# ScalarE makes the D skip of a Mamba-2 mixer in slot 6 of its own chunk instead of slot 3 of the next

## What is computed

```python
zxbcdt = xn @ in_proj_w
z, xBC, dt = split(zxbcdt)                 # 512, 512 + 2*128, 32
dt = softplus(dt + dt_bias)
xBC = silu(causal_conv1d(xBC, conv_w, conv_b))
x_ssm, Bm, Cm = split(xBC)                 # 32 heads of 16
y = ssd_scan(xh, dt, Bm, Cm, A)            # h = h*exp(dt*A) + dt*x*B;  y = h @ C
y = y + D_skip[None, None, :, None] * xh   # the D skip
y = y * silu(z)
y = y * rsqrt(mean(y*y) + 1e-5) * rms_w
return y @ out_proj_w
```

## Time and profile before

| | us |
|---|---|
| median of 3 runs | 3185.61 (3182.48 to 3186.94) |
| the profiled execution, time | 3180.88 |
| the profiled execution, span | 3179.2 |
| PE busy | 2799.2 (88%) |
| DVE busy | 1839.9 (58%) |
| ACT busy | 1384.6 (44%) |
| POOL busy | 678.1 (21%) |
| mean granted clock of PE | 0.943 |

### The profile page before, as it was taken

One profiled execution on the slowest core, in us unless ns is written; L12 is line 12 of the kernel. 1 busy time (PEld: TensorE's weight loads), 2 busy tenths in 40 slices (PEclk: granted clock), 3 DMA queues, 4 the chain that ended last, 5 costly groups with the idle time before them and its releaser, 6 DMA issues. The chain is left out here.

```text
span 3179.2 us, 46142 instructions
## 1 busy us (share of the span) xinstructions
PE 2799.2 (88%) x16998; PEld 2086.3 (66%) x16998; DVE 1839.9 (58%) x3504; ACT 1384.6 (44%) x2394; POOL 678.1 (21%) x716
## 2 busy tenths in 40 slices
PE   0488888888888888869999799999999999999999
PEld 0354555455555555458888687887878787878787
DVE  4688888888888888746767433333333333333332
ACT  0566666666666666536555322222222222222221
POOL 5022222222222222210000122222222222222221
PEclk6799989998999899879999899999999999999999
DMA  3010101010101010035211100000000000000000
GB/s 125 29 35 20 35 20 35 20 35 20 35 21 35 21 35 11 28 104 208 70 62 64 48 13 7 11 14 16 14 16 14 16 14 16 14 16 14 16 14 8
DMA packets 104858, 107.06 MB, mean 34 GB/s; under 512 B 35897, under 2 KB 98617, under 8 KB 102977
## 3 DMA queue, kind: packets, MB, share of 16 engines
q1 hardware_dynamic: 99520, 103.81, 10.1%
q10 hardware_dynamic: 5120, 0.19, 0.1%
HBM read 71.41 MB, written 40.94 MB: 35 GB/s over the span
## 5 line engine op out<-in xcount | busy, mean ns | idle before, releaser
L1597 PE MATMUL fbank<-hid,fw 128*128 128x512 f32 x4096 | 962.3, 395 | 0.0
L1597 PEld LDWEIGHTS fbank<-hid,fw 128*128 128x128 f32 x4096 | 766.1, 187 | 187.0
L1747 DVE TENSOR_TENSOR hid<-fhf,hid 128x512 fp32r<-128x512 f32 x384 | 264.9, 690 | 704.3 <-POOL hid L1704 704.3
L1704 POOL TENSOR_SCALAR hid<-fhf 128x512 fp32r<-128x512 f32 x384 | 271.1, 706 | 1040.2 <-ACT fhf L1676 760.8
L808 ACT ACTIVATE mh<-ebank 128x512 f32<-128x512 f32 x512 | 302.0, 598 | 415.0 <-PE ebank L663 413.8
L1121 DVE SCALAR_TENSOR_TENSOR mh<-mh,gm 128x512 f32<-128x512 f32 x512 | 403.2, 794 | 1.8 <-ACT mh L808 1.8
L663 PE MATMUL ebank<-cright,cleft 102*128 102x512 bf16 x512 | 211.1, 413 | 64.1 <-ACT cin L847 28.9
L1676 ACT ACTIVATE fhf<-fbank,sh2c 128x512 f32<-128x512 f32 x128 | 88.0, 688 | 382.4 <-PE fbank L1597 382.4
L676 PE MATMUL yin<-mh,xpad 128*32 128x128 f32 x4096 | 230.5, 300 | 27.1 <-DVE mh L1121 26.6
L650 PE MATMUL ebank<-ah,win 128*128 128x512 f32 x640 | 246.7, 425 | 7.1 <-ACT cin L847 6.6
L1676 ACT ACTIVATE fhf<-fbank,sh1c 128x512 f32<-128x512 f32 x128 | 88.1, 688 | 320.8 <-PE fbank L1597 320.6
(11 more groups left out here) (180 smaller groups left out, 4380.1 us busy)
## 6 DMA issues: line engine op xcount, KB each, us to landing
fx<-x_d SPq DMA_DIRECT2D x17, 512.0 KB, 3.9
xs<-in_x SPq DMA_DIRECT2D x16, 512.0 KB, 4.3
h_d<-in_h SPq DMA_DIRECT2D x16, 512.0 KB, 5.4
o_d<-o SPq DMA_DIRECT2D x16, 512.0 KB, 2.9
mo<-o_d SPq DMA_DIRECT2D x16, 512.0 KB, 3.8
mx<-in_x SPq DMA_DIRECT2D x16, 512.0 KB, 4.8
x_d<-mx SPq DMA_DIRECT2D x16, 512.0 KB, 2.8
fw<-h_d SPq DMA_DIRECT2D x2, 4096.0 KB, 15.2
```

The lines of the kernel that those rows point to most:

```text
L1597: mm = pe.matmul(bank[banks.slot(key)][:], w[:, k, m * P:(m + 1) * P].bitcast(dt), h[:, k, :].bitcast(dt), start=(k + n == 0), stop=(k == ...
L1704: pool.tensor_scalar(hid[i % 2][0][:, m, :], hf[j % 3][:], 1.0, 0.0, ALU.mult, ALU.add)\
L1747: dve.tensor_tensor(hid[i % 2][1][:, m, :], hf[j % 3][:], hid[i % 2][0][:, m, :].bitcast(F32), ALU.subtract).then_inc(c_lo.sem, 1)
```

## The change

ACT's loop makes the skip of chunk q in slot 6 of chunk q, behind that slot's exponential. Before, it made the skip of chunk q - 1 in slot 3 of chunk q. Nothing else in the program moves. The semaphores and what they count stay the same, so the skip of chunk q now waits for DVE's sum of chunk q - 1, which DVE makes in the same chunk.

```diff
@@ -916,8 +916,8 @@
                     y_out(q - 2)
                 if i == 2 and has_off(q - 1):
                     state_decay(q - 1)
-                if i == 3 and has_chunk(q - 1):
-                    skip(q - 1)
+                if i == 6 and has_chunk(q):
+                    skip(q)
                 if i == 7 and has_chunk(q + 1):
                     b_by_token(q + 1)
                 if j < BLOCKS:
```

## The result

| | before | after |
|---|---|---|
| median of 7 runs, us | 3186.17 (3182.48 to 3198.08) | 3215.44 (3208.78 to 3217.15) |
| ratio, 95% interval | | 1.0078 (1.006 to 1.0096) |
| profiled execution, time and span | 3180.88, 3179.2 | 3217.0, 3215.3 |
| mean granted clock | 0.943 | 0.935 |
| mean block time, from DVE's sums at n = 17 | (1277.92 - 179.99) / 14 = 78.42 | (1310.75 - 188.17) / 14 = 80.18 |

The change makes the kernel slower: by 29 us on the medians, and by 0.8% or 25 us (19 to 31) by the ratio with its interval. The forecast had the sign and a loss of 51. In the profiled executions the difference is 36 us: 8.2 before the first of those sums, 24.6 in the 14 blocks and 3.3 behind. The blocks are the part that the argument was about.

What follows compares the result with a forecast made beforehand. DVE and PE were both taken as near full, with waits deciding. Direct stalls and gains +11, clock falls +49, regained clock -9: +51 us on 3180.9, 3232; the median 4.7 higher, 3237 us; range 3180 to 3285.

Steps and rivals of the forecast that it cites:

- the price of one fall of the clock: One fall of the granted clock, priced from a stretch at 454.0 to 460.9: 2.2 us, at most 3.4.
- the skip removed from n = 3: Slot n = 3: at most 0.3 us come free on DVE, which doesn't end this part; counted 0.
- The stalls: Slots n = 6 and 14: the skip delays the bank reads PE waits for, +1.16 us each, 2.32 a block.
- n = 22: PE's wait grows from 0.29 to 1.45 us, taken up by its 1.18 us wait for POOL; counted 0.
- Reaching the end: At n = 17 DVE already waits 0.31 us for PE, so the 2.32 us pass whole; wait rises over 2.
- rival C: DVE's full queue hides PE's stalls, only the n = 27 gain stays: -23 us, 3162; chance 0.12.
- The clock at the stalls: PE stalls of 2.12 us, twice a block, lower the clock at three of four: 22 times 2.2, +49 us.
- The regained clock: Slow stretch behind the gates: PE, busier there, may get its clock back earlier: -9 us, bounds -18 and 0.
- the forecast 1.56: Slot n = 27: of DVE's 3.85 us of idling, 1.56 us a block reach PE and are gained.
- B: Stalls lengthen but the clock stays up, as the Trainium skill's rule has it: 3188 to 3197, say 3190; chance 0.17.
- D: Either the edit moves nothing on the path, 3186, or ACT waits for DVE at its new place, 3200; chance 0.08.

Runs made afterwards that it cites:

- filled (5): The changed kernel, with PE making the mask product four more times at n = 6 and 14 during its wait: 3188.56 us, ratio 1.0006 to before.
- last in slot (11): Against the kernel before: every skip in slot 6 of its own chunk, behind all other work, the normalisation too: 3136.83 us, ratio 0.9842.
- experiment 2: The kernel before, with only the third chunk's skip moved from n = 27 to n = 22, ahead of the sz copy: 3153.11 us, ratio 0.9893.
- experiment 9: The kernel before, with PE making the decay product three more times at n = 30 in its wait behind the gates: 3181.26 us, ratio 0.9992.
- 3: The kernel before, with only the third chunk's skip moved to n = 22, behind ACT's read of the z bank: 3153.44 us, ratio 0.9901.
- 12: Against the kernel before: skips moved to slot 6 behind the bank reads, but the last chunk's left at n = 3: 3151.93 us, ratio 0.9892.
- 7: The changed kernel, with two skip copies behind the bank reads at n = 6 and 14 and two more PE products there: 3166.52 us, ratio 0.9936.
- experiment 1: The changed kernel, with the skip in slot 6 moved behind ACT's bank reads: 3137.86 us, ratio 0.9841 to the kernel before.
- experiment 6: The changed kernel, with two of the skip's four copies moved behind the bank reads at n = 6 and 14: 3210.16 us, ratio 1.0074 to before.
- experiment 8: The changed kernel, with one skip copy ahead of the bank reads at n = 6 and 14, three behind: 3162.30 us, ratio 0.9925 to before.
- experiment 10: Against the kernel before: each skip in slot 5 of its own chunk, behind all that slot's work: 3140.45 us, ratio 0.9868.

## Why the prediction was right in its sign and wrong in its size

The starts of ACT's exponentials mark the slots. Their distances, as means of 13 blocks of the profiled executions, in us:

| from n to n | before | after | filled (5) | last in slot (11) |
|---|---|---|---|---|
| 6 to 8 | 4.42 | 5.98 | 5.58 | 4.42 |
| 8 to 14 | 13.85 | 14.40 | 13.86 | 13.85 |
| 14 to 16 | 4.50 | 6.97 | 5.58 | 4.50 |
| 16 to 22 | 14.89 | 14.89 | 14.89 | 14.89 |
| 22 to 26 | 10.16 | 10.18 | 10.82 | 10.15 |
| 26 to 27 | 8.27 | 8.27 | 8.27 | 8.27 |
| 27 to 1 of the next block | 11.66 | 9.55 | 9.48 | 9.09 |
| 1 to 6 | 10.79 | 10.06 | 10.06 | 10.06 |

Two terms of the sum failed: the price of one fall of the clock, put at 2.2 us and measured at 1.6 (49 us forecast for 22 falls, 35 measured), and the skip removed from n = 3, put at nothing and measured at 0.73 us a block (11 us of gain).

**The stalls: right.** I had 1.16 us at n = 6 and at n = 14. With the clock kept up, the filled kernel gives 5.58 - 4.42 = 1.16 and 5.58 - 4.50 = 1.08. Over 15 blocks that is 34 to 35 us, as forecast.

**n = 22: right for the change.** 22 to 26 takes 10.18 against 10.16. That is in part luck: behind the same stall of 1.45 us the clock falls in every second block of the filled kernel, which takes 10.82 there, and in five blocks of experiment 2.

**Reaching the end: right, at another place.** I wanted DVE's wait at n = 17 to grow from 0.31 to over 2 us. In the same place of the block it is 0.51 (the second line). DVE meets PE's delay earlier, in rows that I hadn't looked at: 2.16 us for the sum of squares, at 660.94, and 1.83 for the state (the first line).

```profile
665.85 0.69 DVE L1164 TENSOR_TENSOR state<-state,dec 128x512 f32<-128x512 f32 x1 [1.83 <-PE bank L713]
...
669.04 0.69 DVE L1131 TENSOR_TENSOR yin_s<-yin,dx 128x512 f32<-128x512 f32 x1 [0.51 <-PE yin L676]
```

The test that I had named for rival C would thus have pointed the wrong way; the block times settle it.

**The clock at the stalls: right in kind, too dear.** I took 22 falls at 2.2 us, and there are three in two blocks, 22. The number is luck: I had taken three of four without a reason for it. The price is the first step that failed. It came from a fall of 6.9 us, and these last 3.4. Beyond the stalls, the table gives 0.40 at 6 to 8, 0.55 at 8 to 14 and 1.39 at 14 to 16, in sum 2.34 a block, 35 us, 1.6 us a fall. So the term was 35 and not 49, and 14 us of the forecast loss weren't there. The filled kernel got back 27 of the 35; it has a dearer stretch from 22 to 26, 0.64 a block, 10 us.

**n = 3: the second step that failed.** I counted 0 for the skip removed from n = 3, as at most 0.3 us would come free on DVE. The table has 10.79 - 10.06 = 0.73 a block, 11 us. Of it 0.21 is there in every block. The rest is the fall behind n = 3, which three of the 15 blocks have before (12.5 us where the others take 10.27) and none has after. I had used that very fall as my price and not asked whether the change would take it away.

**The regained clock: near in size, not for the reason given.** I had -9 us, at most -18, from a PE that is busier behind the gates. From n = 27 on the gain is 11.66 - 9.55 = 2.11 a block; beyond the forecast 1.56 that is 0.55, 8 us. A part of it is the stretch at 0.50, which no longer reaches 13.7 us. But experiment 9 makes PE as busy in that stretch and gains nothing, so its busy time isn't what shortens it. The runs don't show what does, and that stays open. They show such gains where work is moved: experiments 2, 3, 11 and 12 are 31 to 49 us faster than the kernel before.

The ledger of the change: 35 for stalls, 35 for falls, -43 for what was moved away from n = 27 and 3: +27, where the medians have +29 and the traced pair has 36 with the 8 of the first block. The forecast was 35 + 49 - 32, +51 before rounding of its parts. Both errors, 14 and 11 us, went the same way. The ledger is arithmetic after the fact, and its parts aren't independent: the change came out one step of the two-block time above the kernel before, 157.0 to 160.4.

The rivals: B, that the clock stays up, fell with the trace of the change, which has 22 short falls behind the longer waits, and with experiments 5 and 7, in which filling the waits removes them; the rule of the Trainium skill that B went by doesn't hold for this kernel. C, that DVE hides the stalls, fell with the time, 3215 and not 3162, and with the whole 1.16 and 1.08 us of the filled kernel. Of D, the first half fell with the 78 us between experiment 1 and the change; the second fell with the trace, where ACT never waits before the skip.

The order of two steps in one slot, 78 us, is the largest effect here. A separate forecast for the loss in slot 6 and for the gain of leaving slot 3 would have shown that the best version was neither of the two kernels.

## What to carry to other kernels

When a step is moved into a slot, look at what stands behind it on the same engine: the idle time of ACT lay in front of the exponential, and a step behind it delayed a bank for which PE was already waiting. Moving the same step behind the bank reads turned a loss of 29 us into a gain of 47. Price a stall of PE in two parts, its length and the clock, and let a few harmless repeated products in the wait tell them apart. Look at the other blocks too before putting the whole difference down to the place that was edited.

## What the runs showed of the hardware

Behind waits of PE of 1.54 us in otherwise busy stretches the granted clock went to 0.50 (1.2 GHz) in 15 of 30 places (experiment 6), with waits of 2.12 us in 23 of 30 (the change), behind waits of 1.25 us in one of 30 (experiment 8), and behind filled waits of 1.09 and 1.22 us in none. So the length of a wait alone doesn't decide it.

These falls lasted some 3.4 us, those behind n = 3 in the kernel before and in experiment 1 some 6.8, and the stretch behind the gates 6.7 to 13.6 in the rows shown. A fall of 3.4 us lengthened its block by 1.4 to 1.6 us, and one of 6.8 us by 2.2 to 2.5.

Adding 8 records of matmul work in each of 30 stalls made the changed kernel 27 us faster; filling a wait in a stretch that was already at 0.50 gave nothing (3181.26 against 3184.54).

Experiment 1 had one run of 3157 beside its median of 3138, and experiment 10 two of 3159 beside 3140. Both traces are of such runs and have the fall behind n = 3 in seven blocks. What brings that fall about in one execution and not in the next stays open.
